# Attention by Fourier transform, then a gated low-rank FFN: the normalizer's chain moved to the step's front, row statistics ahead of normalization, the constant row added from PSUM, one ctx block between the x spectra

## The reference

```
def _autocorrelation(Q, K, V):                      # Q = layernorm(x), K = V = ctx; 8 heads, L = 512
    qf = jnp.fft.fft(q, axis=2)
    kf = jnp.fft.fft(k, axis=2)
    corr = jnp.fft.ifft(qf * jnp.conj(kf), axis=2).real
    topk = int(C * np.log(L))                       # 12
    w, idx = jax.lax.top_k(corr.transpose(0, 1, 3, 2), topk)
    w = jax.nn.softmax(w, axis=-1)
    for i in range(topk):
        g = jnp.minimum(idx[:, :, None, :, i] + pos, L - 1)
        out = out + w[:, :, None, :, i] * jnp.take_along_axis(v, g, axis=2)
...
x = x + _L0_xattn_ref(_layernorm(x, axis=-1), ctx_4096, ctx_4096)
x = x + _L0_ffn_ref(_layernorm(x, axis=-1), ...)    # gated low-rank FFN, 64 experts of rank 8, top 16
```

## Time and profile before

| | |
|---|---|
| median of 3 runs | 2369.76 us (2369.35 to 2370.2) |
| profiled execution | 2370.08 us, its span 2368.3 us |
| the 33 attention steps | until about 1513 us of the span |
| busy share of the span | PE 93%, DVE 77%, ACT 52%, POOL 68% |
| busy tenths of DVE in the attention slices | mostly 8 and 9 |
| mean granted clock of TensorE | 0.982 |

### The profile page before, as it was taken

The page is one execution under the profiler, slowest core; times in us unless marked ns, Lnnn a source line. Parts: engine busy times, 40 slices in busy tenths (PEclk is TensorE's granted clock), DMA queues, the critical chain, the costliest instruction groups (busy, mean ns, idle before and its releaser), DMA issues.

```text
span 2368.3 us, 30452 instructions
## 1 busy us (share of the span) xinstructions
PE 2196.6 (93%) x9664; PEld 1473.0 (62%) x9664; DVE 1816.7 (77%) x4059; ACT 1242.0 (52%) x2487; POOL 1606.3 (68%) x1093
## 2 busy tenths in 40 slices
PE   4789989989999989999999997799999999999999
PEld 2445545645655654655555655478777877787787
DVE  6688988988989889889889898775656665555552
ACT  3766666656656656656655544544443444444441
POOL 5789989989989988988989997623333333433330
PEclk9899999999999999999999999899999999999999
DMA  5323223323323323223312215635444444444431
GB/s 202 111 76 134 94 76 128 99 76 112 115 76 112 99 93 110 100 78 110 115 58 80 94 41 203 215 111 169 160 152 160 167 159 154 161 164 159 159 125 54
DMA packets 110419, 287.83 MB, mean 122 GB/s; under 512 B 7136, under 2 KB 7264, under 8 KB 109152
## 3 DMA queue, kind: packets, MB, share of 16 engines
q1 hardware_dynamic: 110304, 286.45, 35.3%
HBM read 219.32 MB, written 67.11 MB: 121 GB/s over the span
## 4 chain that ended last, share of the span: by engine, by line
PE 55%; DVE 28%; issue 8%; ACT 6%; POOL 2%; DMA 1%; DVEq 0%; SPq 0%; ACTq 0%; POOLq 0%
PE out L509 6%; PE out L511 5%; PE out L510 5%; PE z L509 5%; PE z L511 5%; PE z L510 5%; DVE prod L869 4%; PE pair L509 4%; PE pair L511 4%; PE pair L510 4%; DVE pick L917 3%; DVE prod L868 3%; PE tp L521 2%; PE lag L607 2%; DVE e L935 2%
## 5 line engine op out<-in xcount | busy, mean ns | idle before, releaser
L1412 POOL TENSOR_TENSOR rows<-rows,cin 128x1024 f32<-128x1024 f32 x48 | 115.8, 2414 | 364.6 <-DMA rows<-out_dram 289.6
L1371 POOL TENSOR_TENSOR r_f<-prod 128x1024 f32<-128x1024 f32 x128 | 303.9, 2386 | 60.0 <-DVE prod L869 57.8
L634 PE MATMUL pair<-r_f,back 128*128 128x512 f32 x768 | 335.9, 593 | 2.9 <-ACT r_f L1266 2.9
L634 PEld LDWEIGHTS pair<-r_f,back 128*128 128x128 f32 x768 | 143.1, 190 | 171.3 <-issue 171.2
L509 PE MATMUL pair<-w_hi,wts_hi 128*128 128x512 f32 x512 | 211.8, 414 | 25.1 <-DVE prod L869 25.1
L509 PE MATMUL out<-b_hi,zt_hi 128*128 128x512 f32 x512 | 210.3, 411 | 1.6 <-ACT zt_hi L1314 1.5
L1143 ACT ACTIVATE xt_full<-tp 128x512 f32<-128x512 f32 x128 | 76.1, 594 | 250.7 <-PE score_sums L534 132.9
L509 PE MATMUL z<-a_hi,xt 128*128 128x512 f32 x512 | 206.0, 402 | 0.4 <-DVE a_lo L819 0.4
L510 PE MATMUL pair<-w_lo,wts_hi 128*128 128x512 f32 x512 | 204.3, 399 | 0.0
L511 PE MATMUL pair<-w_hi,wts_lo 128*128 128x512 f32 x512 | 204.1, 399 | 0.0
L511 PE MATMUL out<-b_hi,zt_lo 128*128 128x512 f32 x512 | 201.1, 393 | 0.0
(11 more groups left out here) (173 smaller groups left out, 5666.8 us busy)
## 6 DMA issues: line engine op xcount, KB each, us to landing
vf<-in_ctx_dram SPq DMA_DIRECT2D x32, 1024.0 KB, 5.2
out_dram<-att_sb SPq DMA_DIRECT2D x32, 1024.0 KB, 4.5
rows<-out_dram SPq DMA_DIRECT2D x64, 512.0 KB, 3.7
cin<-out_dram SPq DMA_DIRECT2D x64, 512.0 KB, 4.1
xin<-in_x_dram SPq DMA_DIRECT2D x64, 512.0 KB, 3.9
out_dram<-rows SPq DMA_DIRECT2D x64, 512.0 KB, 2.7
xf<-in_x_dram SPq DMA_DIRECT2D x30, 1024.0 KB, 5.6
stat_in<-in_x_dram SPq DMA_DIRECT2D x28, 1024.0 KB, 5.1
```

What stands on the lines that cost most here:

```text
L634: return nc.tensor.matmul(pair_ps[:, bank, :], back[:, 3 * bank + n, :], r_f[:, row, :], start=n == 0, stop=n == 2)
L1371: nc.gpsimd.tensor_tensor(dst, prod[:, slot, 0:2, :], prod[:, slot, 2:4, :], ALU.add).then_inc(add_done, 1)
L1412: nc.gpsimd.tensor_tensor(half, first, second, op).then_inc(c_added, 1)
```

## The change

There are five edits.

1. `later_means` runs at the front of the normalizer step, between `evac_sin(0)` and `evac_sin(1)`, and no longer behind `sums_of`. `invert` and `normalizers` stand behind the first pair of weight products, and no longer behind the second.
2. On ACT, in a normalizer step only, `norm` comes after the row sums and squares.
3. The constant row of the ctx spectrum (L times the last row) was scaled by ACT into SBUF (`dc_last`) and added by POOL. Now ACT writes it into a row of the PSUM bank `lag_ps[0]`, and DVE adds it, in every step, between `evac_sin(0)` and `evac_sin(1)`. The first `corr` of a step waits for that.
4. On TensorE, block 0 of `ctx_negacyclic` stands between `x_spectrum(0)` and `x_spectrum(1)`.
5. A copy of four elements of the chosen weights (L1382, two in each step) moves from POOL to ACT (`middle_copy`).

```
@@ tensor
-                def ctx_negacyclic():
-                    for n in range(4):
+                def ctx_negacyclic(blocks):
+                    for n in blocks:
...
+                        if t == 0:
+                            pe.wait_ge(dc_ready, i + 1)
...
                     ctx_cyclic()
                     x_spectrum(0)
+                    ctx_negacyclic((0,))
                     x_spectrum(1)
-                    ctx_negacyclic()
+                    ctx_negacyclic((1, 2, 3))
@@ vector
+                def add_constant():
+
+                    dve.wait_ge(dc_scaled, i + 1)
+                    dve.wait_ge(prod_ready, prod_x(i, 0) + 1)
+                    dc = v_cyc[cur][0:1, 0, :]
+                    nc.vector.tensor_tensor(dc, dc, lag_ps[0][0:1, :], ALU.add).then_inc(dc_ready, 1)
...
                     evac_sin(0)
+                    if s and r == 3:
+                        later_means(k + 2)
+                    add_constant()
                     evac_sin(1)
...
                     sums_of((0, 1))
-                if s and r == 3:
-                    later_means(k + 2)
...
-                        if n == 1 and s and r == 3:
+                        if n == 0 and s and r == 3:
                             invert(k + 2)
@@ scalar
+                def middle_copy(g, t):
+
+                    both = slice(t, t + 2)
+                    act.wait_ge(weighted, CT * g + t + 2)
+                    nc.scalar.activation(pick[:, both, 0:L:2 * P], e[:, both, 2 * P::-2 * P], ACT.Copy).then_inc(w_folded, 1)
...
                     act.wait_ge(last_loaded, 16 * (i + 1))
                     if not is_step(i, 0):
-                        act.wait_ge(dc_ready, i)
-                    nc.scalar.activation(dc_last[:], v_last[0:1, :], ACT.Copy, scale=float(L)).then_inc(dc_scaled, 1)
+                        act.wait_ge(picked, CT * (i - 1) + 3)
+                    nc.scalar.activation(lag_ps[0][0:1, :], v_last[0:1, :], ACT.Copy, scale=float(L)).then_inc(dc_scaled, 1)
...
-                if i + 2 < GROUPS:
+                if i + 2 < GROUPS and r != 3:
                     norm_inputs(k, r, 2)
                     norm(k, r, 2, range(LT))
...
                     row_sums(i + 2)
                     row_squares(i + 2)
+                if i + 2 < GROUPS and r == 3:
+                    norm_inputs(k, r, 2)
+                    norm(k, r, 2, range(LT))
@@ gpsimd
-                    nc.gpsimd.tensor_copy(pick[:, both, 0:L:2 * P], e[:, both, 2 * P::-2 * P]).then_inc(w_folded, 1)
...
-                    pool.wait_ge(dc_scaled, i + 1)
-                    dc = v_cyc[(r + 1) % 2][0:1, 0, :]
-                    nc.gpsimd.tensor_tensor(dc, dc, dc_last[:], ALU.add).then_inc(dc_ready, 1)
...
-                        if n == 1 and s and r == 3:
+                        if n == 0 and s and r == 3:
                             pool.wait_ge(normed, LT * (i + 2))
                             normalizers(k + 2)
```

More of the change, by code:

```diff
@@ L172, in build_program @@
         xfs[1], vf = sb("xf1", [P, 4, CH]), sb("vf", [P, 4, CH])
-        fwd, v_last, dc_last = sb("fwd", [P, 13, P]), sb("v_last", [P, CH]), sb("dc_last", [1, CH])
+        fwd, v_last = sb("fwd", [P, 13, P]), sb("v_last", [P, CH])
         v_cyc[0], v_neg[0] = sb("v_cyc0", [P, 6, CH]), sb("v_neg0", [P, 6, CH])
         p_f, lags = sb("p_f", [P, 4, CH]), sb("lags", [P, L])
+        sb("apart", [P, CH])
         e, pick = sb("e", [P, CT, L]), sb("pick", [P, CT, L])
@@ L1218, in body @@
                         weigh(i - 1, t)
+                    middle_copy(i - 1, 2)
                 if a:
@@ L1274, in body @@
                         weigh(i, t)
+                    middle_copy(i, 0)
                 if is_step(i, 0):
@@ L1284, in body @@
                         weigh(i, t)
+                    middle_copy(i, 2)
                 if is_step(i, GROUPS):
```

## The result

The changed kernel takes 2376.64 us (median of 8 runs, 2375.81 to 2377.84), the kernel before 2370.11 beside it (8 runs); the ratio is 1.0027, with an interval of 1.0016 to 1.0037. That is 6.5 us slower, where no change, 1.0 us faster, was forecast. It lies inside the range and just above the 2376 that the first case alone was given. The profiled execution took 2376.57 us, with a span of 2374.8. DVE is busy 79% of the span, ACT 53%, POOL 66%, PE 93% as before.

A forecast was written before the change was run, and what follows sets the result against it. DVE was taken to set the step, with one loop through TensorE. Normalizer steps: 43.05 + 5.6 + 0.2 + 1.6 = 50.45 us; six gain 0.6 each, step 26 loses 2.6, leaving 1.0 gained: 2368.8, range 2341 to 2380.

The forecast's parts named there:

- the first case: The forecast's own case, four waits behind GpSimd plus the slow clock: 2362 to 2376 us, chance 0.51.
- ACT's chain: Normalizer steps: with statistics ahead and `shift` early, nothing waits for the exponentials, taking 4.7 us away.
- the prediction's other point: Kernel before, normalizer steps except 26: DVE's wait for the exponentials hid the slow clock's cost, 1.6 us.
- The four turns: `later_means` between the sines: four small operations each wait for one GpSimd operation; `evac_sin(1)` 6.0 us late, 5.6 passed on.
- a free L767: Rival: the chain's `tensor_scalar` does not wait for GpSimd, saving 2.35 us a step: 2352.4 or 2341.2 us, chance 0.29.
- a missed turn: Rival: the chain starts too late for GpSimd's first add, each operation one GpSimd operation later: 16.4 us more, 2385.2.
- The hidden chain: Rival: `later_means` fits into DVE's gap before `evac_sin(1)`, 51.4 us less, 2318.4; chance 0.05.
- The invert and the normalizers: Standing between the first and second weight add, they delay DVE's fourth product pair by 0.2 us per normalizer step.
- The clock: PE idles 5.5 us before the late `evac_sin(1)`, then runs slower: 1.6 us per normalizer step, bounds 0 and 3.2.
- Constant row, block 0 and the copies: These changes cost nothing, hidden in existing waits; ordinary steps stay at 43.05 us.

The follow-up runs named there:

- e2: The kernel before with only ACT's new order in normalizer steps (normalization behind row sums and squares): 2349.6 us, ratio 0.991.
- e3: The changed kernel with the chain of means passed through a PSUM bank, at most one SBUF input per operation, one operation added: 2322.26 us, ratio 0.9791.
- e5: The changed kernel with only the chain's `tensor_scalar` reading its sums from PSUM, by one more reduction: 2355.75 us, ratio 0.993.
- e8: e3 with `invert` and `normalizers` back behind the second pair of weight products: 2318.8 us, ratio 0.9783.
- e6: The changed kernel with six unread matmuls in each normalizer step, ahead of TensorE's wait for `evac_sin(1)`: 2363.89 us, ratio 0.9972.
- e1: The changed kernel without the chain's move and ACT's new order; constant row, block 0 and small copies stay: 2362.36 us, ratio 0.9959.
- e4: The changed kernel with six unread matmuls in each normalizer step, behind TensorE's wait for `evac_sin(1)`: 2414.09 us, ratio 1.0177.
- e7: The changed kernel with chain of means, `invert` and `normalizers` back at their old places, ACT's new order kept: 2336.28 us, ratio 0.9855.

## Why the prediction went wrong

**ACT's chain: right.** 4.7 was taken away; e2 shows it as 4.7 where the clock held. The rest of that run is the prediction's other point, that the wait for the exponentials had swallowed the slow clock: freed of the wait, three of the four steps in which it fell kept 1.6 of it, and the first 2.7.

**The four turns: right**, `tensor_scalar` included. `evac_sin(1)` came 5.83 late for 6.0. e3 and e5 show that it is the operand's place in SBUF that costs a turn. The Trainium skill's page (SBUF — State Buffer, Who interferes with whom), by which both classes of operation contend with GpSimd, agrees with all of this, now for four elements too: 2.39 us from SBUF, 0.15 from PSUM. The rival of a free L767 is excluded by all seven of its rows, that of a missed turn by an L769 of 0.29 (0.58 at most). The hidden chain did not happen as the change is written, but it is what e3 builds: its ratio of 0.9791 makes 2320.6 of 2370.1, some 2 us above the rival's figure.

**The invert and the normalizers: 0.2 forecast, 0.5 measured** (e3 against e8). The steps without the slow clock are 49.24 in the mean (e6), 6.19 above an ordinary one, where 5.6 and 0.2 were forecast. In e6's step 18 the first weight product comes 5.6 later than in an ordinary step, so the turns cost what was forecast. The rest is the fourth product's wait for GpSimd's add, 0.83 there and more in steps 22 and 26 (1.18 and 1.06), instead of 0.36 for PE; why it is longer in these two was not asked.

**The clock: this is the step that failed.** "I put 1.6 on each of the seven", with bounds of 0 and 3.2; it is 2.34 in the mean (e6). The 1.6 were taken from step 26 alone, where the clock was low for only a part of the work behind the gap: 0.53 over 3.4 us and 0.72 over 6. In the changed kernel it is 0.50 over 5.7 us in step 18, which hold the transposes, all of the first `corr` and part of the weight spectra. 5.7 us of work at half speed are 2.85 of delay, of which 2.44 reach the step's end. The term was mis-sized by 0.74, in seven steps 5.2 us. With the 0.39 above, 2.7 more, that is 7.9, and the first output's end 0.6 earlier leaves 7.3 of the 7.5 by which the forecast was missed.

The higher price stood in the trace of before. In its steps 2 and 22 the clock was 0.50 over the 3.4 us behind the gap and 0.50 to 0.52 over 6, and the third product waited 3.23 us, 2.46 more than in step 18. These are the windows and the timeline of step 22:

```profile
1048.80:1052.20 3.40, 3.39 (x8) 2.72 (x9) 2.31 (x3) 0.00 (x0) 3.30 (x2) 0.50 0.00 0
```

```profile
1054.34 1.23 DVE L866 SCALAR_TENSOR_TENSOR prod<-pair,v_cyc 128x1024 f32<-128x1024 f32 x1 [3.23 <-PE pair L511]
```

The gaps ahead of these were as long as the others of before, 3.1 to 3.2 us. So what sets the price is how much of the work behind the gap runs at the lower clock, and a gap of 3.1 to 3.3 us left either amount (steps 22 and 26 of before, steps 18 and 26 of e5). In the changed kernel, behind 5.3 us and more, the clock was 0.51 to 0.64 over 6 us in all seven. What decides between the two amounts was not tested.

**Constant row, block 0 and the copies: "nothing" held for the ordinary steps** (43.03). It did not hold for the edits by themselves: with the chain at its old place they shorten the normalizer steps by 7 us together (e1), since GpSimd's folds move and the chain meets the second half of one operation and not the whole. With edit 1 that gain can't be had, because the chain has left the place. The prediction asked only what these edits cost, not which wait their shift of GpSimd would shorten.

**The sum.** By edits the whole comes to: edits 3 to 5 about 10 us faster, edit 2 21 faster alone, all four together 34 faster (0.9855), and edit 1 41 slower on top of that. The net of +6.5 is the difference of two large terms, so that a miss of a tenth in one of them, 3 to 4 us, is more than the 1.0 us gain that was forecast.

## What to carry to other kernels

Before small DVE operations are moved into a gap, look at what GpSimd does there, not at the gap's length alone: here each link of a dependent chain paid one GpSimd operation, and the same chain with at most one operand in SBUF (none for the `tensor_scalar`) paid nothing. When a wait grows on DVE, look at how long PE idles for it, and price the clock by the work that runs at the lower clock behind it. Take all instances of a gap in the trace, the dearest ones too, and not one of them. A few matmuls that nobody reads, issued ahead of the wait, kept the clock here. An edit that changes when GpSimd's operations begin has to be priced at each place where a DVE operation waits for them, for gains as well as losses.

## What the runs showed of the hardware

- A `tensor_scalar` of 128 x 4 in fp32 with its input in SBUF took 2.386 to 2.396 us beside GpSimd's adds in all seven steps, and 0.156 to 0.158 where no GpSimd operation followed the one just ending (e1), or 0.148 to 0.150 beside its adds with the input in PSUM (e5).
- Both engines took turns, operation by operation: DVE's four small operations ended with GpSimd's four large ones (856.03, 858.38, 860.67, 862.97), and an operation of DVE that came 0.17 us after a fold had begun waited for the fold's end, 2.19 us in all.
- Idle stretches of PE and the clock behind them: 5.3 to 5.6 us, 1.2 GHz behind it in seven of seven (changed kernel, e4); 3.1 to 3.3 us, in six of seven before, five of seven in e2 and seven of seven in e5; 2.0 to 2.3 us, in four of seven in e1 and two of seven in e7; 1.4 to 1.7 us, the wait of the later blocks of `ctx_negacyclic` for `evac_sin(0)` in the steps up to 30 of the changed kernel, and none behind it. Six matmuls in the longest gap kept 2.4 GHz in all seven steps (e6).
